# Attention's causal mask: added on VectorE with the row maximum in all four query blocks, no longer by TensorE in two of them

## The reference, cut to what matters

```python
q = (x @ wq).reshape(b, s, NH, HD)
k = (x @ wk).reshape(b, s, NKV, HD)
v = (x @ wv).reshape(b, s, NKV, HD)
scores = jnp.einsum('bihd,bjhd->bhij', q, k) * SCALE
scores = jnp.where(causal, scores, jnp.finfo(scores.dtype).min)
attn = jax.nn.softmax(scores, axis=-1)
out = jnp.einsum('bhij,bjhd->bihd', attn, v)
return out @ wo
```

## Time and profile before

| | us |
|---|---|
| median of 3 runs | 895.54 (894.24 to 896.49) |
| the profiled execution | 893.8 |
| its span, first to last instruction | 892.0 |

### The profile page before, as it was taken

One profiled execution on the slowest core, in us unless ns is written; L12 is line 12 of the kernel. 1 busy time (PEld: TensorE's weight loads), 2 busy tenths in 40 slices (PEclk: granted clock), 3 DMA queues, 4 the chain that ended last, 5 costly groups with the idle time before them and its releaser, 6 DMA issues.

```text
span 892.0 us, 13693 instructions
## 1 busy us (share of the span) xinstructions
PE 847.3 (95%) x5096; PEld 674.2 (76%) x5096; DVE 678.1 (76%) x1068; ACT 535.9 (60%) x721; POOL 194.0 (22%) x200
## 2 busy tenths in 40 slices
PE   3999999999997988899999999999999999999998
PEld 1556777777676777788888887788877888888886
DVE  4836889889978778598888776677886867667852
ACT  3413776778745342866666576677556876666840
POOL 3003567778663224000000000000220000000004
PEclk9998999999999999999999999999999999999999
DMA  9778778897651033025433333133312443332202
GB/s 322 239 221 156 82 110 144 126 141 92 141 177 36 1 82 87 33 78 151 111 105 110 103 98 95 48 95 97 93 48 73 140 118 95 96 95 71 72 1 95
DMA packets 38450, 95.35 MB, mean 107 GB/s; under 512 B 7144, under 2 KB 10216, under 8 KB 37360
## 3 DMA queue, kind: packets, MB, share of 16 engines
q1 hardware_dynamic: 35840, 90.68, 41.9%
q10 hardware_dynamic: 2544, 3.79, 1.2%
HBM read 79.56 MB, written 2.21 MB: 92 GB/s over the span
## 4 chain that ended last, share of the span: by engine, by line
PE 58%; DVE 9%; ACT 3%; issue 2%; POOL 1%; DVEq 0%; ACTq 0%; POOLq 0%
PE PS L1730 12%; PE PS L1731 12%; PE PS L1732 12%; PE PS L2054 6%; PE PS L2056 6%; PE PS L2055 6%; DVE ACC L1313 1%; DVE ST L1232 1%; POOL X L813 1%; ACT XM L917 1%; PE PS L2039 1%; DVE SCR L1298 1%; PE PS L2027 1%; PE PS L1986 1%; DVE XN L1247 1%
## 5 line engine op out<-in xcount | busy, mean ns | idle before, releaser
L948 ACT ACTIVATE PL<-CODE 128x1024 f32<-128x1024 int32 x200 | 202.2, 1056 | 60.9 <-DVE ACC L1313 58.3
L1730 PE MATMUL PS<-HH,WRH 128*128 128x512 f32 x448 | 175.2, 391 | 2.7 <-DVE HL L1267 2.6
L1731 PE MATMUL PS<-HH,WRL 128*128 128x512 f32 x448 | 174.5, 390 | 0.0
L1732 PE MATMUL PS<-HL,WRH 128*128 128x512 f32 x448 | 174.3, 389 | 0.0
L813 POOL TENSOR_TENSOR X<-X,SCR 128x512 f32<-128x512 f32 x31 | 41.6, 1350 | 539.1 <-DVE SCR L1298 538.6
L1313 DVE SCALAR_TENSOR_TENSOR ACC<-PL,ACC 128x1024 f32<-128x1024 f32 x100 | 123.8, 1238 | 8.2
L996 ACT ACTIVATE PT<-PS 128x512 f32<-128x512 f32 x160 | 87.3, 608 | 37.2 <-PE PS L1855 24.8
L830 POOL TENSOR_TENSOR QS<-ident,MX 64x256 fp32r<-64x256 f32 x128 | 97.7, 763 | 49.5 <-DVE MX L1478 30.2
L1730 PEld LDWEIGHTS PS<-HH,WRH 128*128 128x128 f32 x448 | 84.1, 188 | 22.4 <-DVE HL L1267 3.6
L1732 PEld LDWEIGHTS PS<-HL,WRH 128*128 128x128 f32 x448 | 84.1, 188 | 17.6
L1731 PEld LDWEIGHTS PS<-HH,WRL 128*128 128x128 f32 x448 | 84.2, 188 | 16.7
(11 more groups left out here) (243 smaller groups left out, 1515.5 us busy)
## 6 DMA issues: line engine op xcount, KB each, us to landing
CODE<-in_CODES SPq DMA_DIRECT2D x50, 512.0 KB, 3.5
SCALE<-in_SCALES SPq DMA_DIRECT2D x100, 256.0 KB, 4.0
WM<-in_WM SPq DMA_DIRECT2D x12, 1024.0 KB, 7.3
QS<-FQ SPq DMA_DIRECT2D x32, 256.0 KB, 6.5
KS<-KHL SPq DMA_DIRECT2D x32, 64.0 KB, 5.3
KN<-KHL SPq DMA_DIRECT2D x32, 64.0 KB, 4.5
GAB<-gates SPq DMA_DIRECT2D x4, 512.0 KB, 3.7
out_x<-X ACTq DMA_DIRECT2D x8, 256.0 KB, 2.0
```

The source lines that it names most:

```text
L948: nc.scalar.activation(PL[:, n % 3], CODE[:, p % 2], ACT.Prelu, scale=scale, bias=bias, alpha=alpha).then_inc(s_plane, 1)
L1730: nc.tensor.matmul(dst, lh, rh, start=start and k == 0, stop=False)
L1731: nc.tensor.matmul(dst, ll, rh, start=False, stop=False)
L1732: ins = nc.tensor.matmul(dst, lh, rl, start=False, stop=stop and k == KC - 1)
```

## The change

`ADDED_MASK` gets the blocks 2 and 3. `scores` then issues no mask product at all, and VectorE uses the masked instruction for every block. The loads, semaphores and all other lines stay.

```diff
@@ -90,7 +90,7 @@
 STEPS = len(CAPS) + 1
 
 
-ADDED_MASK = (0, 1)
+ADDED_MASK = (0, 1, 2, 3)
 
 
 PACK_AT = {2 * pair + 5: pair for pair in range(B * PAIRS - 2)}
```

## The result

| | before | after |
|---|---|---|
| median | 895.10 us (10 runs, 893.63 to 896.49) | 898.17 us (10 runs, 896.44 to 899.22) |
| ratio | | 1.0033, 95% interval 1.0023 to 1.0043 |
| profiled execution / its span | 893.8 / 892.0 | 898.3 / 896.5 |
| PE busy, instructions | 847.3 us, 5096 | 842.4 us, 4968 |
| DVE busy, instructions | 678.1 us, 1068 | 686.8 us, 1260 |

The changed kernel is 3.1 us slower. TensorE has the 128 instructions less and is busy 4.9 us less, VectorE 8.7 us more (8.3 was forecast).

A forecast was written before the change was run, and what follows sets the result against it. A ring of VectorE and TensorE work bounds the attention loop. Its passages add 2.2 (six), 0.2 (four), -0.2 (two) and 0 us (three), in sum +2.2 on the median 895.54: 897.7 us, range 892.5 to 902.

The forecast's parts named there:

- VectorE's price: Blocks 2 and 3: add-and-maximum instead of `reduce_max` costs VectorE 0.52 us more a group, 8.3 us over 16 groups.
- the ring: Attention loop: VectorE's work from block 2 to releasing next block 1's scores, then TensorE's order to block 2, sets the time.
- The refund: Block 2: without mask products the score products end sooner and VectorE starts its maxima 0.16 us earlier a group.
- the second pair of block 3: TensorE's score products there: 0.74 us with masks, 0.55 without, a saving of 0.2 us.
- The six plain ones: Passages from one group's block 2 to the next's without a VectorE pause: 0.36 us longer each, 2.2 us together.
- The four that absorb: Passages 3 to 4, 8 to 9, 9 to 10, 13 to 14: pauses absorb most, leaving 0.05 us each, 0.2 together.
- The two with the long pause: Passages 4 to 5 and 7 to 8, VectorE pausing long ahead of block 0: -0.1 us each, -0.2 together.
- The ends: First group starts 0.16 us earlier, last ends 0.06 us later; these nearly cancel.
- three get 0: Passages 0 to 1, 1 to 2, 5 to 6: VectorE idles for other reasons, so no time is added.
- VectorE throughout: Rival: VectorE binds the whole loop, no pause absorbs and nothing is refunded; +8.3 us, 903.8 us; chance 0.12.
- Faster: Rival: wide instructions add under 0.16 us a group, so shorter score products win; about -4.5 us, 891 us; chance 0.15.
- Absorbed: Rival: loop pauses swallow more or heads cost 0.1 us a group less; +0.3 us, 895.8 us; chance 0.25.

The follow-up runs named there:

- e1: Kernel before, with VectorE's add-and-maximum in blocks 2 and 3 while TensorE keeps its mask products there: ratio 1.0063, median 900.3 us.
- e2: Kernel before, with TensorE's mask products for the maxima of blocks 2 and 3 dropped, VectorE keeping `reduce_max`: ratio 0.9963, median 891.6 us.
- e3: Kernel before, with the exchange in block 2 alone (`ADDED_MASK = (0, 1, 2)`): ratio 1.0021.
- e4: Kernel before, with the exchange in block 3 alone (`ADDED_MASK = (0, 1, 3)`): ratio 1.0021.
- g1: Changed kernel, but group 0 keeps blocks 2 and 3 as before: ratio 1.0031 against before, +2.9 us.
- g2: Kernel before, with the exchange in block 3 of group 0 alone, one block of 64: ratio 1.0011, +1.1 us.
- f1: Kernel before, with VectorE's decoding sum moved from behind block 3 of even groups to behind block 1 of odd ones: ratio 0.9956.
- g4: The kernel of f1 run and profiled once more, with more rounds: ratio 0.9952 against before.

## Why the prediction was right

*Size and sign.* +2.2 us and 897.7 were forecast; +3.1 by the medians and 898.17 measured, inside the range, and 0.9 us above the likeliest case. The prediction's bound of 0.3% (2.7 us) lies within the interval of the measured ratio, 1.0023 to 1.0043, so its choice between "same" and "slower" isn't decided. The loop, which was to be 2 us longer, is 3.4 us longer in the two profiles.

*VectorE's price.* 0.52 us a group forecast; measured 2.03 - 1.74 = 0.29 and 2.56 - 2.28 = 0.28, 0.57. e1 shows it on the ring: 0.58.

*The refund.* 0.16 us a group forecast, 0.17 by e1 against the change, 0.19 by e2. That the estimated 14 us of TensorE's work would be worth little is what e2 shows: 3.6 us. For the second pair of block 3 the prediction's terms, twice 0.24 and 0.1 for the first load, add up to 0.58 and not to 0.55; measured was 0.57, and no run shows the 0.1 by itself.

*The classes of passages.* The six plain ones: 6 x 0.36 = 2.2 forecast, 0.42, 0.41, 0.41, 0.22, 0.46 and 0.67 measured, 2.6 in all. The four that absorb: +0.2 forecast, -0.02, +0.32, -0.05, -0.45 measured, -0.2; that the sum comes near is partly luck, for they spread from -0.45 to +0.32 around a forecast of +0.05 each, and 9-10 came to -0.05 by +0.18 (e3) and -0.24 (e4) and not by a pause that absorbs. The two with the long pause: -0.2 forecast, -0.1 measured. The ends: -0.1 forecast, +0.1.

*The step that failed* is "three get 0". Passages 1-2 and 5-6 gave +0.07 and -0.39 (the latter by the transfer that happened to come in time), but 0-1 gave +1.26. I had set a fall of the clock aside since it was 1.00 in both stretches that I had read, and neither of them held the loop's start. Nor did TensorE's pauses stay as they were: the longest wait of its weight loads for L1474 went from 1.1 to 1.8 us. In the profiles of g1 and g2 the passage is long with the exchange in block 3 of group 0 and not without, and in every such profile the low clock reaches into group 1's block 1. Why the low stretch moves is open; that TensorE is busy 3.49 us of the stretch from 81 to 86 us instead of 4.79 is what the profile shows. How much of it is in the medians stays open, since g1 did not differ from the change beyond the interval. Without the three passages the profiles' loops differ by 2.5 us, with them by 3.4, and the 3.1 of the medians lies between.

*The rivals.* "VectorE throughout" (+8.3) fell with e1, where nothing was refunded and the cost was still 5 us. "Faster" fell: two wide heads cost 0.14 us more than the `reduce_max` that they replace, not under 0.04. "Absorbed" fell with the passages. The rule that the prediction takes from the Trainium skill (Perfetto Trace Analysis, Identifying the Most-Contended Engine) pointed to VectorE, and burdening it did cost time, but 3.1 us and not 8.3; and relieving the other engine was worth 3.6 us (e2).

## What to carry to other kernels

When two engines hand one pair of buffers back and forth, read start-to-start distances along one period and mark which instructions lie on the ring; the price of an exchange is what it adds on the ring less what it takes off it, and here 0.17 of the added 0.58 us came back although TensorE was relieved of more than VectorE was given (an estimated 14 us against 8.7). The same reading says what to move: a decoding sum shifted from the ring into a pause brought some 4 us with no work saved, in the kernel before; in the changed one, whose VectorE has hardly a pause left, it brought about 0.5. Read the period at the loop's start too, where the pipeline fills, before taking one from the middle for all.

## What the runs showed that I had not expected

- The lower clock costs by where it falls and not by its length alone: 6.8 us of it in group 0 went with 0.87 us more in passage 0-1 (f1 against g4, one kernel), and 3.4 us of it in group 1's block 1 with 1.2 us more (g2 against before).
- The add-and-maximum keeps one slope from 128 to 512 columns: 318, 450 (before), 588 and 724 ns (after), 132 to 138 ns for each 128 columns.
- The transfer of the row sums `RC<-DEN` behind the codes lands late by up to 2.6 us in one place of the loop, and passage 5-6 varies from 10.43 to 12.09 us between kernels.
